# Second attention: the quotient's numerators kept and divided in place in a ring of five units, and its row sums formed one slot group later

## The chip, the cores and the metric

One core of a Trainium2 chip runs the whole program in one launch. The metric is device time in microseconds (us) of that core; lower is better. The kernel before took 3159.86 us (median of 3 runs, 3156.14 to 3160.17).

## The reference, cut to what matters

The program is one hybrid layer on x of shape (4, 512, 512): a first attention with a pairwise sparsity mask, a feed-forward block, a second (differential) attention, the feed-forward block again. Only the second attention is touched. It computes, for each batch b and head h of 16:

```python
attn1 = einsum('bthd,bshd->bhts', q1, k1) * scale
attn2 = einsum('bthd,bshd->bhts', q2, k2) * scale
score = softmax(attn1 - lam * attn2, axis=-1)
out = einsum('bhts,bshd->bthd', score, v)
out = (1.0 - LAMBDA_INIT) * out.reshape(B, T, E)
x = x + out @ W_proj
```

## The kernel before, in words

Each of the five engines (TensorE, VectorE, ScalarE, GpSimd, SyncE) gets its own instruction stream from one list of steps, which `order_of_attention_b` (lines 1778 to 1893) writes out; `attention_b` (lines 1896 to 2274) walks the list and every engine's program emits its share of each step. So the position of a step in the list is its position in each engine's queue.

Work is cut into 16 units: 4 batches times 4 groups of 4 heads (`HU` = 4). A unit has 16 score tiles of 128 x 512. For each tile there are two products: one (`max_b`, matmul L2065, then a row maximum on VectorE, L2168) finds the maxima, and one (`exp_b`, matmul L2080, then the exponential on ScalarE, L2236) gives exp(score - max) transposed. The maxima pass of unit n runs one unit ahead of the exponentials. The list is made in slots, 16 to a unit: slot i of block n holds the exponentials' tile (n-1, i-6) (from i = 6; the slots 0 to 5 still belong to unit n-2), the maxima's tile (n, i), at slots 10, 14, 2 and 6 a `weighted_b` step, and at most one half of a side step. In what follows "slot i" is this i, "class" is n mod 4.

The steps around the change:
- `weighted_b` (t = 0 to 3): 8 matmuls of 32 columns each (L2091) accumulate v times exponentials in one PSUM bank. After t = 3 ScalarE copies this bank, the numerators, to SBUF (L2242).
- GpSimd adds the exponentials over the four t into `ex_sum` (L2018); the adds of the next unit with t = 1 wait until the sums' matmuls have read it (`sums_done`).
- `sums_b`: 8 matmuls of 32 columns against ones (L2103) turn `ex_sum` into row sums, spread over the heads' partitions; ScalarE copies them to SBUF (L2246).
- `divide_b`: 8 pieces of 128 x 64, each a reciprocal (L2177) and a product (L2178) on VectorE, into `out_t`; one piece per odd slot, or in every slot where the block's class is 1.
- `project_b`: for t = 0 to 3 a product with `W_proj` (L2114), in two halves, two slots behind the division of its pieces, once per batch; VectorE adds it to x (L2184).
- `product_b` (L2050), `values_b` (L2038), `turn_b` (L2027) make the queries, keys, values and turned inputs of units to come, in two banks (`SIDE`) that all side steps use in turn; ScalarE makes `hi_b` from a product (L2218) and VectorE `lo_b` (L2160), and SyncE sends both (`send_b`, L2261 and L2265). `place_b` at slot 2 turns the maxima on TensorE (L2072), copies them on ScalarE (L2224), which then issues four DMAs (L2229).

Before, the numerators go to `sums_sb[:, 0]`, the sums to `sums_sb[:, 1]`, and the quotients to `out_t[:, c]`, c = 0 to 3. The numerators' copy therefore waits for the previous unit's last division, and a batch's first division for the previous batch's last projection:

```python
act.wait_ge(divided, 2 * NT * n)          # L2241, before the copy L2242
dve.wait_ge(proj_done, NT * b)            # L2176, before the reciprocal L2177
```

The sums step enters the side queue one slot behind the last weighted sums (slot 7, or slot 8 where a half step is open), the unit's first division right behind it:

```python
if step[2] == NT - 1 and step[1] < UNITS - 1:
    held.insert(0, (m + 1, ("sums_b", step[1])))
```

Behind the last unit, the list ends with `early_b` (the first three quarters of the last batch's projection, L2126), the last weighted sums, sums, divisions and `last_b` (L2131, L2190). `early_b` waits for all divisions of unit 14. The second feed-forward block starts when the last x is added.

Of the kernel before, what the change touches and what calls it, by code (L numbers as in the profile page):

```python
# [7 lines left out]
ACT = mybir.ActivationFunctionType  # L8
# [7 lines left out]
P = 128  # L16
B, S, D = 4, 512, 512
NT = S // P
ND = D // P
# [3 lines left out]
HB, HDB = 16, 16  # L23
# [1749 lines left out]
UNITS_B = HB // HU  # L1773
UNITS = B * UNITS_B
# [3 lines left out]
def order_of_attention_b():  # L1778
    order, side, light, divisions, due, half_done, held = [], [], [], [], [], [], []

    def norms(b):
        return [("norm_b", b, t) for t in range(NT)]

    def turned_steps(b):
        return [("turn_b", b, f) for f in range(ND)] + [("values_b", b, t) for t in range(NT)]

    def divide(n, piece, m):

        order.append(("divide_b", n, piece))
        if n % UNITS_B == UNITS_B - 1 and piece % 2:  # L1790
            held.append((m + 2, ("project_b", n // UNITS_B, piece // 2)))

    def advance():
        if half_done:
            step = half_done.pop()
            order.append((*step, 1))
            if step[0] == "project_b":
                light.append(("stats_b", step[1], step[2]))
            return
        step = side.pop(0)  # L1800
        if step[0] in ("values_b", "product_b", "project_b"):
            order.append((*step, 0))
            half_done.append(step)
            return
        order.append(step)
        if step[0] == "sums_b":
            n, = step[1:]
            divisions.extend((n, piece) for piece in range(2 * NT))
            if n == UNITS - 1:
                divisions.clear()  # L1810
                last = iter([("divide_b", n, piece) for piece in range(2 * NT)])
                order.extend([("early_b", 2), next(last), next(last), next(last), next(last)])
                for t in range(NT):
                    order.append(("last_b", t))
                    order.extend([("early_b", 3)] if t == 0 else [("stats_b", B - 1, t - 1)])
                    order.extend(step for step in (next(last, None), next(last, None)) if step)
                order.append(("stats_b", B - 1, NT - 1))

    def query_key_steps(n):
        return [("product_b", n, 0), ("product_b", n, 1), ("send_b", n)]  # L1820

    order += norms(0)
    side, due = turned_steps(0)[:ND], turned_steps(0)[ND:]
    while side:
        advance()
    side += query_key_steps(0)
    advance()
    order.append(("query_scale",))
    side += query_key_steps(1)
    while side or half_done:  # L1830
        advance()
    side, due = due[:NT // 2], due[NT // 2:]
    while side or half_done:
        advance()
    order.append(("load_projection",))
    order += norms(1)
    rows, own, sums = iter(()), iter(()), iter(())
    query_key = []
    for m in range(TILES * (UNITS + 1) + LAG + HU + 4):
        n, i = m // TILES, m % TILES  # L1840
        if i == 0 and n < UNITS:
            rows = iter([("max_b", n, j) for j in range(TILES)])
            if n % UNITS_B == 0 and n // UNITS_B + 1 < B:
                due += turned_steps(n // UNITS_B + 1)
            share = 0 if n == 0 else NT // 2 + ND if n == 1 else (ND, 0, NT // 2, NT // 2)[n % UNITS_B]
            if n < 2:
                side, query_key = query_key_steps(2)[:3 * (n == 0)] + side, []
            else:
                query_key = query_key_steps(n + 1) if n + 1 < UNITS else []
            side = query_key[:2] + side + due[:share]  # L1850
            due = due[share:]
        if i == TILES // 2 and n % UNITS_B == UNITS_B - 1 and n // UNITS_B + 2 < B:
            light += norms(n // UNITS_B + 2)
        if i == LAG + 1:
            side[:0] = query_key[2:]
            query_key = []
        if i == LAG and 1 <= n <= UNITS:
            own = iter([("exp_b", n - 1, t, g) for t in range(NT) for g in range(HU)])
        if i == (LAG + HU) % TILES and 1 <= n <= UNITS:
            sums = iter([("weighted_b", n - 1, t) for t in range(NT)])  # L1860
        while held and held[0][0] <= m:
            step = held.pop(0)[1]
            if step[0] == "sums_b":
                side.insert(0, step)
            else:
                side.append(step)
        order += [step for step in (next(own, None),) if step]
        if i == 2 and 1 <= n <= UNITS:
            order.append(("place_b", n - 1))
        order += [step for step in (next(rows, None),) if step]  # L1870
        if (i - LAG - HU) % HU == 0:
            step = next(sums, None)
            if step:
                if step[1:] == (UNITS - 1, NT - 1):
                    order += [("early_b", 0), step, ("early_b", 1)]
                else:
                    order.append(step)
                if step[2] == NT - 1 and step[1] < UNITS - 1:
                    held.insert(0, (m + 1, ("sums_b", step[1])))
                elif step[2] == NT - 1:  # L1880
                    side.insert(0, ("sums_b", step[1]))
        if side or half_done:
            advance()
        if divisions and (i % 2 or n % UNITS_B == 1):
            divide(*divisions.pop(0), m)
        if light and (i % 2 == 0 or i < NT):
            order.append(light.pop(0))
    while side or light or half_done:
        if light:
            order.append(light.pop(0))  # L1890
        else:
            advance()
    return order


def attention_b(k):
    nc, d, ps, x = k.nc, k.d, k.ps, k.x
    pe, dve, act, pool, sp, chain = k.pe, k.dve, k.act, k.pool, k.sp, k.dve_chain
    signal = k.flag
    ROWS, N_EX, SCALE = 97, 10, HDB ** -0.5  # L1900
    O1_BANKS, O2_BANKS, SUM_BANK, SIDE = (0, 1, 2), (3, 4), 5, (6, 7)
    LAST_BANKS = O1_BANKS + O2_BANKS[:1]
    order = order_of_attention_b()
# [46 lines left out]
    with ExitStack() as mem:  # L1950
# [10 lines left out]
        v = sb(mem, "vb", [P, 2, NT, D])  # L1961
        ex = sb(mem, "ex_b", [P, N_EX, S])
        ex_sum = sb(mem, "ex_sum", [P, HU, S])
        out_t = sb(mem, "out_t", [P, ND, S])
        sums_sb = sb(mem, "sums_sb", [P, 2, S])
        maxes = sb(mem, "maxes_b", [P, 2, HU, NT])
        max_t = sb(mem, "max_t_b", [HU, 2, S], F32R)
        ones = sb(mem, "ones_b", [P, 32])
# [51 lines left out]
        def tensor(kind, *at):  # L2020
# [85 lines left out]
            elif kind == "project_b":  # L2106
# [4 lines left out]
                    pe.wait_ge(proj_weights, 16)  # L2111
                    side_free(step[:3])
                for c in range(2 * half, 2 * half + 2):
                    s = nc.tensor.matmul(ps[:, bank, :], out_t[:, c, t * P:t * P + P], w_proj[:, c, :], start=c == 0,  # L2114
                                         stop=c == ND - 1)
                if half:
                    s.then_inc(proj_done, 1)
            elif kind == "early_b":
# [4 lines left out]
                if t == NT - 1:  # L2123
                    pe.wait_ge(ex_made, TILES * UNITS)
                for c in range(ND - 1):
                    nc.tensor.matmul(ps[:, LAST_BANKS[t], :], out_t[:, c, t * P:t * P + P], w_proj[:, c, :], start=c == 0,  # L2126
                                     stop=False)
            elif kind == "last_b":
                t, = at
                pe.wait_ge(divided, 2 * NT * (UNITS - 1) + 2 * t + 2)  # L2130
                nc.tensor.matmul(ps[:, LAST_BANKS[t], :], out_t[:, ND - 1, t * P:t * P + P], w_proj[:, ND - 1, :],  # L2131
                                 start=False, stop=True).then_inc(proj_done, 1)

        def vector(kind, *at):
            step = (kind, *at)
# [35 lines left out]
                add_exponentials(dve, nc.vector, ex_added_last, *at, HU // 2, 0)  # L2171
            elif kind == "divide_b":
                n, piece = at
                b, c, part = n // UNITS_B, n % UNITS_B, slice(piece * P // 2, piece * P // 2 + P // 2)
                dve.wait_ge(sums_made, n + 1)
                dve.wait_ge(proj_done, NT * b)  # L2176
                chain(nc.vector.reciprocal(sums_sb[:, 1, part], sums_sb[:, 1, part]))  # L2177
                nc.vector.tensor_tensor(out_t[:, c, part], sums_sb[:, 0, part], sums_sb[:, 1, part],  # L2178
                                        ALU.mult).then_inc(divided, 1)
            elif kind == "project_b" and at[2]:  # L2180
                b, t, half = at
# [15 lines left out]
        def scalar(kind, *at):  # L2197
# [40 lines left out]
            elif kind == "weighted_b" and at[1] == NT - 1:  # L2238
                n, t = at
                act.wait_ge(weighted_done, NT * n + NT)  # L2240
                act.wait_ge(divided, 2 * NT * n)  # L2241
                nc.scalar.activation(sums_sb[:, 0, :], ps[:, SUM_BANK, :], ACT.Copy).then_inc(out_sums, 1)  # L2242
            elif kind == "sums_b":
                n, = at
                act.wait_ge(sums_done, n + 1)
                nc.scalar.activation(sums_sb[:, 1, :], ps[:, side_bank[step], :], ACT.Copy).then_inc(sums_made, 1)  # L2246

        def gpsimd(kind, *at):
            if kind == "exp_b" and (at[0] < UNITS - 1 or at[2] >= HU // 2):
# [88 lines left out]
```

## Time and profile before

| what | value |
|---|---|
| median of the runs | 3159.86 us |
| lowest, highest run | 3156.14, 3160.17 us |
| span of the profiled execution, first to last instruction | 3157.4 us |
| PE, DVE, ACT, POOL busy over the span | 95%, 74%, 56%, 34% |
| mean granted TensorE clock, share of full speed | 0.976 |
| second attention in the span | about 2124 to 2622 us |

The profile gives the span of one execution and no separate total for it; the span is 2.5 us under the median of the runs. PE is the matmul part of TensorE, PEld its weight loads, DVE is VectorE, ACT ScalarE, POOL GpSimd, SP SyncE; a "q" behind an engine means its DMA queue. Busy shares count the modelled time of matmuls, which overlap. "Idle before, releaser" is idle time of that engine directly before an instruction and what ended it.

### The profile page before, as it was taken

How to read it: one execution, taken by the hardware profiler on the slowest of the kernel's cores; microseconds unless marked ns; L12 is line 12 of the kernel's file. 1: busy time of each engine (PE TensorE's matmuls, PEld its weight loads, DVE VectorE, ACT ScalarE, POOL GpSimd, SP SyncE). 2: the span in 40 equal slices, each digit the busy share in tenths (PEclk: the TensorE clock that was granted, in tenths of full speed). 3: DMA queues.
4: the chain of work that ended last, by engine and by line, in shares of the span. 5: the costliest groups of instructions: out<-in, count | busy, mean ns of one | idle time of the engine just before them, and what ended most of it. 6: DMA issues, size and time to landing. Idle time of an engine off the chain costs nothing. (4 is left out here: it accounts for less than half of the span.)

```text
span 3157.4 us, 45069 instructions
## 1 busy us (share of the span) xinstructions
PE 3004.7 (95%) x16681; PEld 1670.8 (53%) x16681; DVE 2335.5 (74%) x4298; ACT 1771.7 (56%) x2897; POOL 1059.2 (34%) x881
## 2 busy tenths in 40 slices
PE   6999999999999899999899989989999987999999
PEld 3334334333433344444478868854444435887787
DVE  6988998999898877777366676655766776667665
ACT  4988888888888546666633333323443443334332
POOL 1000000000000264543155565613545554565653
PEclk9999999999999889999999999999999988999999
DMA  2000000000000000000111111124333311112111
GB/s 75 1 1 11 1 1 11 1 1 11 1 1 1 1 1 2 1 2 1 31 44 54 50 41 57 47 92 109 88 91 77 101 34 53 44 54 74 54 53 44
DMA packets 105759, 112.18 MB, mean 36 GB/s; under 512 B 8963, under 2 KB 74500, under 8 KB 105157
## 3 DMA queue, kind: packets, MB, share of 16 engines
q1 hardware_dynamic: 102918, 108.61, 12.2%
q8 instruction: 134, 2.20, 0.3%
q10 hardware_dynamic: 2624, 0.69, 0.1%
q14 instruction: 83, 0.68, 0.1%
HBM read 84.76 MB, written 20.97 MB: 33 GB/s over the span
## 5 line engine op out<-in xcount | busy, mean ns | idle before, releaser
L730 DVE TENSOR_SCALAR pair_in<-key_words,row_words 128x512 f32<-128x512 f32 x1792 | 726.1, 480 | 44.7 <-PE ps L617 40.7
L815 ACT ACTIVATE pair_mid<-ps,row_bias 128x512 f32<-128x512 f32 x896 | 588.2, 688 | 133.5 <-PE ps L617 116.1
L617 PE MATMUL ps<-pair_in,w_hi 128*64 128x512 f16 x3584 | 584.7, 390 | 8.6 <-DVE pair_in L730 8.3
L1081 DVE TENSOR_REDUCE maxes<-ps 128x2 f32<-128x1024 f32 x256 | 303.2, 1221 | 94.5 <-PE ps L994 93.4
L843 POOL TENSOR_SCALAR_AFFINE_SELECT sim<-sim 128x512 f32<-128x512 f32 x16 | 9.9, 620 | 1051.9 <-ACT sim L832 1051.9
L617 PEld LDWEIGHTS ps<-pair_in,w_hi 128*64 128x64 f16 x3584 | 202.3, 108 | 301.8 <-issue 66.4
L617 PE MATMUL ps<-pair_in,w_lo 128*64 128x512 f16 x1792 | 352.3, 388 | 0.0
L1491 PE MATMUL ps<-ffn_b_hi,ffn_a_hi 128*128 128x512 f32 x904 | 287.6, 400 | 24.8 <-DVE ffn_up L1579 9.9
L1125 ACT ACTIVATE ex<-ps 128x512 f32<-128x512 f32 x448 | 243.2, 595 | 118.2 <-PE ps L1013 117.4
L1491 PE MATMUL ps<-ffn_b_lo,ffn_a_hi 128*128 128x512 f32 x904 | 283.5, 395 | 2.4 <-DVE ffn_b_lo L1561 2.4
L1491 PE MATMUL ps<-ffn_b_hi,ffn_a_lo 128*128 128x512 f32 x904 | 282.8, 394 | 0.7 <-POOL ffn_a_lo L1722 0.7
L1629 DVE TENSOR_TENSOR x<-x,ps 128x512 f32<-128x512 f32 x256 | 175.5, 686 | 138.6 <-PE ps L1508 135.5
L631 PE MATMUL ps<-pair_mid,w_slide 128*32 128x512 f32 x2048 | 246.2, 598 | 0.0
L2236 ACT ACTIVATE ex_b<-ps 128x512 f32<-128x512 f32 x256 | 147.1, 599 | 171.7 <-PE ps L2080 170.5
L2168 DVE TENSOR_REDUCE maxes_b<-ps 128x1 f32<-128x512 f32 x256 | 169.4, 682 | 86.1 <-PE ps L2065 85.6
L1491 PEld LDWEIGHTS ps<-ffn_b_hi,ffn_a_hi 128*128 128x128 f32 x904 | 170.0, 191 | 70.8 <-DVE ffn_up L1579 12.4
L1722 POOL TENSOR_TENSOR ffn_a_lo<-ffn_sums,ffn_a_hi 128x1024 fp32r<-128x1024 f32 x60 | 148.3, 2471 | 171.2 <-ACT ffn_a_hi L1644 171.2
L1689 ACT ACTIVATE ffn_gate<-ffn_gate 128x512 f32<-128x512 f32 x60 | 37.9, 632 | 278.6 <-DVE ffn_gate L1586 278.6
L1491 PEld LDWEIGHTS ps<-ffn_b_lo,ffn_a_hi 128*128 128x128 f32 x904 | 172.1, 191 | 40.8 <-DVE ffn_b_lo L1561 4.2
L1491 PEld LDWEIGHTS ps<-ffn_b_hi,ffn_a_lo 128*128 128x128 f32 x904 | 172.4, 191 | 37.9 <-POOL ffn_a_lo L1722 1.1
L2018 POOL TENSOR_TENSOR ex_sum<-ex_sum,ex_b 128x512 f32<-128x512 f32 x124 | 156.2, 1276 | 85.9 <-ACT ex_b L2236 85.6
L1722 POOL TENSOR_TENSOR ffn_a_lo<-ffn_raw_up,ffn_a_hi 128x512 fp32r<-128x512 f32 (+1 forms) x128 | 136.6, 1089 | 105.9 <-PE ps L1045 67.0
(240 smaller groups left out, 5344.6 us busy)
## 6 DMA issues: line engine op xcount, KB each, us to landing
ffn_raw_up<-in_w_ffn SPq DMA_DIRECT2D x64, 512.0 KB, 4.0
ffn_raw_down<-in_w_ffn SPq DMA_DIRECT2D x64, 256.0 KB, 2.7
q_stack<-halves SPq DMA_DIRECT2D x48, 256.0 KB, 5.1
k_stack<-halves SPq DMA_DIRECT2D x48, 256.0 KB, 5.9
halves<-hi_b SPq DMA_DIRECT2D x16, 512.0 KB, 2.7
halves<-lo_b SPq DMA_DIRECT2D x16, 512.0 KB, 3.6
out<-x SPq DMA_DIRECT2D x4, 1024.0 KB, 4.5
x<-in_x SPq DMA_DIRECT2D x6, 512.0 KB, 6.9
```

The lines of the kernel that those rows point to most:

```text
L617: s = nc.tensor.matmul(ps[F2 * half:F2 * half + F2, bank + which, :], w_part[:, :], words.rearrange("p (s two) -> p s two", two=2)[:, :, o ...
L631: s = nc.tensor.matmul(ps[32 * c:32 * c + 32, 6 + w, :], p.w3_slide[:, 30 - 2 * r:62 - 2 * r], p.pair_mid[:, n % NG, half, :], start=r == ...
L730: s = nc.vector.tensor_scalar(p.pair_in[:, (4 * n + i) % N_PAIR, :], p.key_words[:, b % 2, :], p.row_words[:, b % 2, row:row + 1], None, A ...
L815: nc.scalar.activation(p.pair_mid[:, n % NG, which, :], ps[:, bank + which, :], ACT.Relu, bias=bias).then_inc(p.mid_made, 1)
L1081: nc.vector.tensor_reduce(maxes[:, c % 2, 2 * pair:2 * pair + 2, h], ps[:, 2 * pair:2 * pair + 2, :], AX.X, ALU.max).then_inc(maxes_made, 1)
L1125: nc.scalar.activation(ex[:, i % N_EX, :], ps[:, EXP_BANKS[j], :], ACT.Exp, scale=2.0 ** -0.5).then_inc(ex_made, 1)
L1491: i = nc.tensor.matmul(bank, a_part[:, s % 2, a_at, h, :], b_part[:, place(operand), h, :], start=opens and (which, m, h) == (0, 0, 0), st ...
L1629: nc.vector.tensor_tensor(x[:, n, :], x[:, n, :], ps[:, 6 + t % 2, :], ALU.add).then_inc(x_added, 1)
L1722: nc.gpsimd.tensor_tensor(lo, source, hi.bitcast(F32), ALU.subtract).then_inc(w_lo_made, 1)
L2018: engine.tensor_tensor(ex_sum[:, g, :], first, ex[:, i % N_EX, :], ALU.add).then_inc(done, 1)
L2168: nc.vector.tensor_reduce(maxes[:, n % 2, g, t:t + 1], ps[:, O1_BANKS[i % 3], :], AX.X, ALU.max).then_inc(max_made, 1)
L2236: nc.scalar.activation(ex[:, i % N_EX, :], ps[:, O2_BANKS[i % 2], :], ACT.Exp, scale=SCALE).then_inc(ex_made, 1)
```

## The change

The numerators' copy writes straight into `out_t`, which now has 5 rows of units in a ring; the division works in place there. `sums_sb` keeps the sums alone. The numerators' copy waits no longer for divisions but, from unit 5 on, for the projection that read its place in the ring. The sums' copy now waits for the previous unit's last division, and every division also for its numerators' copy. The `sums_b` step of unit n leaves the side queue and stands directly behind `weighted_b` (n+1, t = 0), at slot 10; the divisions follow from there. For the last unit `sums_b` stays where it was. SBUF in use is the same (4 + 2 rows before, 5 + 1 after).

```diff
@@ order_of_attention_b
         if step[0] == "sums_b":
             n, = step[1:]
-            divisions.extend((n, piece) for piece in range(2 * NT))
             if n == UNITS - 1:
-                divisions.clear()
                 last = iter([("divide_b", n, piece) for piece in range(2 * NT)])
...
         while held and held[0][0] <= m:
-            step = held.pop(0)[1]
-            if step[0] == "sums_b":
-                side.insert(0, step)
-            else:
-                side.append(step)
+            side.append(held.pop(0)[1])
...
-                if step[2] == NT - 1 and step[1] < UNITS - 1:
-                    held.insert(0, (m + 1, ("sums_b", step[1])))
-                elif step[2] == NT - 1:
+                if step[2] == 0 and step[1] > 0:
+                    order.append(("sums_b", step[1] - 1))
+                    divisions.extend((step[1] - 1, piece) for piece in range(2 * NT))
+                if step[1:] == (UNITS - 1, NT - 1):
                     side.insert(0, ("sums_b", step[1]))
@@ attention_b
-    ROWS, N_EX, SCALE = 97, 10, HDB ** -0.5
+    ROWS, N_EX, N_OUT, SCALE = 97, 10, UNITS_B + 1, HDB ** -0.5
...
-        out_t = sb(mem, "out_t", [P, ND, S])
-        sums_sb = sb(mem, "sums_sb", [P, 2, S])
+        out_t = sb(mem, "out_t", [P, N_OUT, S])
+        sums_sb = sb(mem, "sums_sb", [P, S])
...
-                b, c, part = n // UNITS_B, n % UNITS_B, slice(piece * P // 2, piece * P // 2 + P // 2)
+                part, out = slice(piece * P // 2, piece * P // 2 + P // 2), out_t[:, n % N_OUT, :]
+                dve.wait_ge(out_sums, n + 1)
                 dve.wait_ge(sums_made, n + 1)
-                dve.wait_ge(proj_done, NT * b)
-                chain(nc.vector.reciprocal(sums_sb[:, 1, part], sums_sb[:, 1, part]))
-                nc.vector.tensor_tensor(out_t[:, c, part], sums_sb[:, 0, part], sums_sb[:, 1, part],
+                chain(nc.vector.reciprocal(sums_sb[:, part], sums_sb[:, part]))
+                nc.vector.tensor_tensor(out[:, part], out[:, part], sums_sb[:, part],
                                         ALU.mult).then_inc(divided, 1)
...
                 act.wait_ge(weighted_done, NT * n + NT)
-                act.wait_ge(divided, 2 * NT * n)
-                nc.scalar.activation(sums_sb[:, 0, :], ps[:, SUM_BANK, :], ACT.Copy).then_inc(out_sums, 1)
+                if n >= N_OUT:
+                    act.wait_ge(proj_done, NT * ((n - N_OUT) // UNITS_B + 1))
+                nc.scalar.activation(out_t[:, n % N_OUT, :], ps[:, SUM_BANK, :], ACT.Copy).then_inc(out_sums, 1)
             elif kind == "sums_b":
                 n, = at
                 act.wait_ge(sums_done, n + 1)
-                nc.scalar.activation(sums_sb[:, 1, :], ps[:, side_bank[step], :], ACT.Copy).then_inc(sums_made, 1)
+                act.wait_ge(divided, 2 * NT * n)
+                nc.scalar.activation(sums_sb[:, :], ps[:, side_bank[step], :], ACT.Copy).then_inc(sums_made, 1)
```

The projections (`project_b`, `early_b`, `last_b`) read `out_t` at the unit's number modulo 5 in place of c.

## Rows read from the trace of the kernel before

**Rows 1.** The page's head and first part: span, busy time by engine.

```profile
span 3157.4 us, 45069 instructions
...
PE 3004.7 (95%) x16681; PEld 1670.8 (53%) x16681; DVE 2335.5 (74%) x4298; ACT 1771.7 (56%) x2897; POOL 1059.2 (34%) x881
```

**Rows 2.** Busy time by stretch; columns: stretch, length, PE, PEld, DVE, ACT, POOL, clock, DMA, GB/s.

```profile
2124.00:2622.00 498.00, 465.57 (x1732) 203.22 (x1730) 340.70 (x599) 199.50 (x361) 234.31 (x186) 0.96 0.32 83
```

**Rows 3.** Waits in the second attention: who waited for whom, total us, times, longest.

```profile
ACT sums_sb L2242 <- DVE out_t L2178: 25.8, 7, 4.3
...
PE ps L2080 <- ACT ex_b L2236: 10.7, 16, 2.1
DVE sums_sb L2177 <- PE ps L2114: 10.1, 2, 5.1
...
PE ps L2065 <- DVE maxes_b L2168: 6.7, 11, 1.3
```

**Rows 4.** Timeline at the numerators' copies; columns: start, us, engine, line, [idle before].

```profile
2212.51 0.60 ACT L2242 ACTIVATE sums_sb<-ps 128x512 f32<-128x512 f32 x1 [4.28 <-DVE out_t L2178]
...
2237.57 1.07 PE L2103 MATMUL ps<-ex_sum,ones_b 128*32 128x512 f32 x8
...
2239.54 0.60 ACT L2242 ACTIVATE sums_sb<-ps 128x512 f32<-128x512 f32 x1 [3.30 <-DVE out_t L2178]
...
2241.17 0.50 PE L2080 MATMUL ps<-q_stack,k_stack 97*128 97x512 f32 x1 [1.86 <-ACT ex_b L2236]
```

**Rows 5.** Timeline of PE: other idle stretches of over 0.8 us, by what ended them.

```profile
2312.44 0.50 PE L2065 MATMUL ps<-k_stack,q_stack 96*128 96x512 f32 x1 [0.86 <-DVE maxes_b L2168]
...
2365.81 0.51 PE L2080 MATMUL ps<-q_stack,k_stack 97*128 97x512 f32 x1 [1.86 <-ACT ex_b L2236]
...
2486.63 0.50 PE L2080 MATMUL ps<-q_stack,k_stack 97*128 97x512 f32 x1 [2.11 <-ACT ex_b L2236]
...
2564.97 0.64 PE L2103 MATMUL ps<-ex_sum,ones_b 128*32 128x512 f32 x4 [0.86 <-POOL ex_sum L2018]
...
2584.81 0.64 PE L2103 MATMUL ps<-ex_sum,ones_b 128*32 128x512 f32 x4 [1.14 <-POOL ex_sum L2018]
```

**Rows 6.** Busy time by stretch, as rows 2: behind or around three of these idles.

```profile
2243.00:2246.00 3.00, 3.00 (x12) 1.04 (x12) 0.93 (x3) 0.65 (x3) 1.27 (x1) 0.54 1.06 207
...
2364.00:2368.00 4.00, 2.19 (x16) 1.25 (x16) 2.07 (x6) 3.81 (x8) 0.00 (x0) 1.00 0.88 197
...
2487.00:2490.00 3.00, 2.76 (x12) 0.50 (x10) 1.98 (x4) 1.65 (x4) 0.94 (x1) 0.68 1.07 197
```

**Rows 7.** Timeline: one slot without and one with weighted sums, both with side work.

```profile
2274.35 0.80 PE L2080 MATMUL ps<-q_stack,k_stack 97*128 97x512 f32 x1
...
2276.55 0.80 PE L2080 MATMUL ps<-q_stack,k_stack 97*128 97x512 f32 x1
...
2279.93 0.80 PE L2080 MATMUL ps<-q_stack,k_stack 97*128 97x512 f32 x1
```

**Rows 8.** Timeline: from the sums of unit 3 to the first projection.

```profile
2265.75 0.60 ACT L2246 ACTIVATE sums_sb<-ps 128x512 f32<-128x512 f32 x1 [0.78 <-PE ps L2103]
...
2268.28 0.22 DVE L2178 TENSOR_TENSOR out_t<-sums_sb 128x64 f32<-128x64 f32 x1
...
2268.56 1.98 PE L2114 MATMUL ps<-wb_proj,out_t 128*128 128x512 f32 x4
...
2273.95 1.13 DVE L2178 TENSOR_TENSOR out_t<-sums_sb 128x64 f32<-128x64 f32 x1
```

**Rows 9.** Timeline: slot 2 of block 6, maxima placed between two products.

```profile
2287.83 0.75 DVE L2160 SCALAR_TENSOR_TENSOR lo_b<-ps,q_scale,hi_b 128x512 fp32r<-128x512 f32 x1 [1.68 <-ACT hi_b L2218]
...
2288.78 2.43 ACTq L2229 DMA_DIRECT2D q_stack<-max_t_b  x4
...
2288.91 1.98 PE L2050 MATMUL ps<-zb_t,wb_qk 128*128 128x512 f32 x4
```

**Rows 10.** Timeline: PE reaches the end of the last unit.

```profile
2601.66 2.84 PE L2126 MATMUL ps<-wb_proj,out_t 128*128 128x512 f32 x6
```

More of the change, by code:

```diff
@@ L2113, in tensor @@
                 for c in range(2 * half, 2 * half + 2):
-                    s = nc.tensor.matmul(ps[:, bank, :], out_t[:, c, t * P:t * P + P], w_proj[:, c, :], start=c == 0,
-                                         stop=c == ND - 1)
+                    s = nc.tensor.matmul(ps[:, bank, :], out_t[:, (UNITS_B * b + c) % N_OUT, t * P:t * P + P],
+                                         w_proj[:, c, :], start=c == 0, stop=c == ND - 1)
                 if half:
@@ L2125, in tensor @@
                 for c in range(ND - 1):
-                    nc.tensor.matmul(ps[:, LAST_BANKS[t], :], out_t[:, c, t * P:t * P + P], w_proj[:, c, :], start=c == 0,
-                                     stop=False)
+                    nc.tensor.matmul(ps[:, LAST_BANKS[t], :], out_t[:, (UNITS - UNITS_B + c) % N_OUT, t * P:t * P + P],
+                                     w_proj[:, c, :], start=c == 0, stop=False)
             elif kind == "last_b":
@@ L2130, in tensor @@
                 pe.wait_ge(divided, 2 * NT * (UNITS - 1) + 2 * t + 2)
-                nc.tensor.matmul(ps[:, LAST_BANKS[t], :], out_t[:, ND - 1, t * P:t * P + P], w_proj[:, ND - 1, :],
-                                 start=False, stop=True).then_inc(proj_done, 1)
+                nc.tensor.matmul(ps[:, LAST_BANKS[t], :], out_t[:, (UNITS - 1) % N_OUT, t * P:t * P + P],
+                                 w_proj[:, ND - 1, :], start=False, stop=True).then_inc(proj_done, 1)
         def vector(kind, *at):
```

## The prediction

> **What bounds the kernel now.** First the page's head: the span, and which engine is busy [rows 1]. TensorE is busy for 95% of 3157.4 us, so only what lengthens or shortens its stream counts. Then the table by stretch, cut to the second attention [rows 2]: 465.6 of 498 us of TensorE, 340.7 of VectorE, 199.5 of ScalarE. Even here TensorE is the limit, and 498 - 465.6 = 32 us is all its idle time. The change touches no other stage, and the feed-forward block starts when the last x is added, so a microsecond won or lost here is one of the total.
>
> Then the waits [rows 3]. ScalarE waits 25.8 us in 7 pieces for the last division before it may copy the numerators: the largest wait that the change aims at. It is not a gain of 25.8 us. TensorE has its own price of it: it idled 10.7 us in 16 pieces for exponentials. The timeline shows how [rows 4]. At 2212.51, after a wait of 4.28 us, no idle stands on TensorE: it had value products to do. At 2239.54 the same wait of 3.30 us stops it for 1.86 us, since there was no side work but the sums. The same comes back at 2365.81 (1.86) and 2486.63 (2.11) [rows 5]. So of seven waits three reach TensorE, with 5.83 us. The second wait is that of VectorE for the last projection of the batch before, 10.1 us in 2 pieces; behind it the maxima come late, and TensorE idles 0.86 us at 2312.44, the first of four rows alike (two each in blocks 6 and 10, 0.86 to 0.91 us), some 3.5 us out of the 6.7 us of maxima waits [rows 3, 5]. The third is the sums' own wait for GpSimd's adds, 2.0 us in 2 pieces (0.86 and 1.14) [rows 5].
>
> **The change, part by part.**
>
> *Numerators' copy without the wait for divisions.* It takes away 5.83 us of idle at most. ScalarE must still make its 0.60 us copy there, and in slots without side work TensorE runs at ScalarE's pace of one 0.6 us exponential a slot; the sums, which filled part of this time with 1 us of matmuls [rows 4], are no longer there. I take 1.5 us for each of the three, 4.5 us; bounds 3.0 (half) and 5.8. The other four waits give nothing: with side work TensorE is late itself.
>
> *Clock.* Behind two of the three stops the granted clock falls to its lower level (1.2 in place of 2.4 GHz) for part of the next 3 us: means 0.54 and 0.68 [rows 6]. At full speed these stretches hold 3.0 x 0.46 and 3.0 x 0.32 us more, 2.3 us together. Without the stop before them I take 2.0 us; bounds 0 and 3.1, as the fall behind 2487 goes on past its row.
>
> *Divisions without the wait for the projection.* The ring takes away the 10.1 us of VectorE, and with it TensorE's 3.5 us; I take 3.5, bounds 1.7 and 3.5.
>
> *Sums three slots later.* GpSimd's last add of a unit is then several slots old, so both waits for it go: 2.0 us, bounds 1.0 and 2.0. The new cost is on GpSimd: its adds with t = 1 of the next unit start only when the sums are through, some 2 us later than their exponentials. Twelve adds of 1.26 us (234.3 us for 186 [rows 2]) are 15.1 us in a unit of at least 20 us (the last ones, 2565 to 2585 in [rows 5]), and the places they free are wanted six slots later. Cost 0, hidden by GpSimd's 34% load [rows 1]; without that cover the next sums would wait 1:1.
>
> *Two groups of narrow matmuls back to back.* A slot with weighted sums starts its successor 3.38 us later (2276.55 to 2279.93), one without after 2.20 (2274.35 to 2276.55) [rows 7]: a group costs 1.18 us, while its matmuls fill 1.07 [rows 4] and are started over about 1.0. Merged, a second group should cost about 1.0: 0.2 us each for 14 units, 2.8 us; bounds 0 and 4.6 (0.33 each, its entry without side work). The Trainium skill, TensorEngine Tiling (Array Packing), section Key Properties, says that changing the tiling mode drains TensorE, while changing the tile does not; by it each merged pair saves a whole change of mode, and the sum would stand at the upper bound. No row here has two such groups in a row.
>
> *Projection (new wait 1).* For n = 3, 7, 11 the first two divisions follow the sums at once, and the projection stands two slots behind its division, as before. Before, TensorE had after the sums three pairs of score products and the weighted sums, and it arrived at 2268.56, just as the second quotient (2268.28 + 0.22) was ready, 2.75 us after the sums' copy had started (2265.75) [rows 8]. Now the weighted sums stand ahead of the sums, so TensorE arrives 1.0 us earlier and waits; and GpSimd starts its held-back adds at the same moment, under which a product of 128 x 64 takes 1.13 us in place of 0.22 [rows 8]. Cost 1.2 us for each of 3; bounds 0 and 2.4 (both products delayed), so 3.6 us, 0 to 7.2.
>
> *Side steps shift by one slot (new wait 2).* With divisions from slot 10, projection 0 starts at slot 13 and the second half of projection 1 takes slot 0 of the next block (6, 10, 14). So the query product takes slots 1 and 2 and not 0 and 1, and `place_b`, fixed at slot 2, stands before its second half. On ScalarE the maxima's copy and four DMA issues of 2.43 us (2288.78) then stand before the `hi_b` copy, where they stood behind it [rows 9]. The key product shares its bank with the query product and waits for `lo_b`: the issues end at 2291.2, a copy of this size takes 0.60 [rows 4], `lo_b` 0.75 [rows 9], so with the hand-overs between engines `lo_b` ends near 2292.8 and the matmul could start at 2293.1. TensorE arrives one half product and two score products behind 2288.91, 2.2 us by the plain slot [rows 7], at 2291.1. Cost 2.0 us for each of 3, 6.0 us; bounds 0 and 6.6. Before, no idle stood here (2288.91). SyncE's sends move to slot 7 or 8, one or two earlier: no cost.
>
> *Sums' copy waits for divisions; divisions for numerators.* The last division stands at slot 9 or before, the copy needs matmuls that end about 3 us into slot 10: cost 0, with a VectorE lag under 2 us as cover. If VectorE is later than that, ScalarE's exponentials queue behind the copy. The numerators' copy is four slots old when wanted: 0. Copy and product in place have the shapes of before: 0.
>
> *The tail.* Unit 14's divisions end two slots later, at the slot before `early_b` (0), which stands at 2601.66 [rows 10] and waits for them; VectorE also adds for unit 15 there. The idle of 1.14 us before it is counted above. I take 0; bounds 1.5 us of gain (no wait for GpSimd, denser matmuls and a better clock) and 2 us of loss.
>
> **Sum.** Gains 4.5 + 2.0 + 3.5 + 2.0 + 2.8 = 14.8 us; losses 3.6 + 6.0 = 9.6 us; net 5.2 us faster. The profiled span of 3157.4 would be 3152.2; against the median of the runs, 2.5 us above the span, 3154.7.
>
> **Rivals.** *A, new waits are covered.* If `lo_b` and the first quotients come in time (VectorE is idle for a third of the stage [rows 2]), the gains stand alone: 3159.9 - 14.8 = 3145 us, with half of a wait left 3149. For it: before, both places are met to within 0.1 us. Against it: ScalarE is blocked by its own DMA issues, and that doesn't hinge on load. Chance 0.15.
>
> *B, the wait moves.* ScalarE's wait is not removed but moved to the sums' copy, and where no side work stands TensorE runs at ScalarE's pace anyway; the gains of the first two parts go, and the rest cancels against the new waits: 8.3 against 9.6 us, 3159.9 +- 2. For it: four of seven waits cost nothing even now. Against: the last division, which released the copy at 2239.54 [rows 4], falls in slot 9, and the new wait stands some 3 us into slot 10. Chance 0.20.
>
> *C, slower.* One mechanism: TensorE's new stops at the projection and the key product, in blocks 5, 6, 9, 10, 13 and 14, let the granted clock fall, as stops of 1.9 and 2.1 us did in two of three cases [rows 5, 6]. A fall costs about 1.5 us (3 us at half rate). Six of them are 9 us: 3154.7 + 9 = 3163.7. It decides from the point where more than three or four of the six stops fall so. Against: these blocks are full of side work, and at 2365.81 the clock stayed up [rows 6]. The Trainium skill, TensorE: Matmul & The Clock Gate, section Part 1, has the clock set by how busy the engine recently was; the rows agree that the falls stand behind stops. Chance 0.15.
>
> **Numbers.** The forecast case (net gain between 2 and 9 us) has 0.50. A measurement of this kernel tells about 0.2% from no change, 6.3 us, so the case lies on both sides of that line: 0.28 faster, 0.22 same. Faster: 0.28 + 0.15 (A) = 0.43. Same: 0.22 + 0.20 (B) + 0.03 of C = 0.45. Slower: 0.12. The range of 3146 to 3163 us takes in the forecast case, most of A and B and half of C.
>
> **What would show it.** Right: no wait of L2242 for L2178 and none of L2177 for L2114; no idle over 1 us at slot 9 of blocks 4, 8 and 12; no wait of L2103 for GpSimd except in the last unit; clock at full level behind these places; the two narrow groups together at about 2.0 us. New: TensorE idle of 1 to 2.4 us before the first L2114 of batches 0 to 2, and about 2 us before the key product L2050 of blocks 6, 10 and 14. Wrong: a wait of L2246 for L2178 of several us (B), or the second attention as long as before with the clock's mean under 0.95 (C), or neither new wait there (A).

## The result and the profile after

The changed kernel took 3170.99 us (median of 5 runs, 3166.78 to 3172.22) against 3159.86 before; the ratio is 1.0034, 95% interval 1.0022 to 1.0047. It is slower by 0.34%, where 5 us less were forecast, and outside the range.

The page's head and first part, as [rows 1]:

```profile
span 3169.4 us, 45086 instructions
...
PE 2999.3 (95%) x16681; PEld 1673.1 (53%) x16681; DVE 2339.6 (74%) x4298; ACT 1773.6 (56%) x2897; POOL 1061.1 (33%) x881
```

No engine has more to do; the 12 us are waiting time and time at the lower clock. The table by stretch over the same window as [rows 2] (stretch, length, PE, PEld, DVE, ACT, POOL, clock, DMA, GB/s):

```profile
2124.00:2622.00 498.00, 453.42 (x1703) 203.61 (x1701) 334.65 (x574) 198.46 (x358) 234.38 (x186) 0.96 0.32 82
```

TensorE works 12.2 us less in these 498 us than before: the stage now ends later (its last projection starts at 2633.38 and not at 2619.50), so less of it lies in the window. The waits of the stage (who, for whom, total us, times, longest), as [rows 3]. L2075 is the exponentials' matmul (L2080 before), L2060 the maxima's (L2065), L2109 the projection (L2114), L2121 `early_b` (L2126), L2098 the sums (L2103), L2013 GpSimd's adds (L2018), L2173 the division's product (L2178):

```profile
POOL ex_sum L2013 <- PE ps L2098: 102.4, 14, 10.5
...
ACT ex_b L2231 <- POOL ex_sum L2013: 14.5, 12, 2.6
...
PE ps L2060 <- DMA k_stack<-halves: 10.3, 4, 4.3
...
PE ps L2075 <- ACT ex_b L2231: 8.6, 17, 2.2
...
PE ps L2109 <- DVE out_t L2173: 6.4, 3, 2.1
...
PE ps L2045 <- DVE lo_b L2155: 5.8, 5, 1.4
PE ps L2060 <- DVE maxes_b L2163: 5.5, 8, 1.3
...
PE ps L2121 <- DVE out_t L2173: 5.2, 1, 5.2
```

The waits that the change was to remove are gone: no numerators' copy waits for a division, no reciprocal for a projection, and no sums for GpSimd. In their place stand three that were not there or small: the operands' DMA 10.3 us (1.5 before), the first projections 6.4 (0 before), the end 5.2 (0 before). The timeline of PE shows where (start, us, engine, line, [idle before]):

```profile
2248.18 0.53 PE L2060 MATMUL ps<-k_stack,q_stack 96*128 96x512 f32 x1 [2.69 <-DMA k_stack<-halves]
...
2272.46 2.93 PE L2109 MATMUL ps<-wb_proj,out_t 128*128 128x512 f32 x3 [2.14 <-DVE out_t L2173]
2291.54 1.98 PE L2045 MATMUL ps<-zb_t,wb_qk 128*128 128x512 f32 x4 [1.19 <-DVE lo_b L2155]
...
2377.28 0.80 PE L2060 MATMUL ps<-k_stack,q_stack 96*128 96x512 f32 x1 [4.32 <-DMA k_stack<-halves]
...
2572.23 0.50 PE L2075 MATMUL ps<-q_stack,k_stack 97*128 97x512 f32 x1 [1.54 <-ACT ex_b L2231]
...
2613.98 2.08 PE L2121 MATMUL ps<-wb_proj,out_t 128*128 128x512 f32 x2 [5.19 <-DVE out_t L2173]
```

The projection's stop comes back at 2401.97 and 2525.24 (2.13 each), the key product's at 2421.25 and 2544.24 (1.39, 1.19), the DMA's at 2502.67 (2.40). And behind some of the stops the clock falls, in the table by stretch of the 3 or 4 us that follow each:

```profile
2248.00:2251.00 3.00, 2.82 (x4) 1.28 (x5) 2.15 (x5) 0.00 (x0) 1.97 (x2) 0.59 0.00 0
...
2273.00:2276.00 3.00, 3.00 (x5) 1.07 (x4) 1.98 (x6) 0.00 (x0) 0.55 (x1) 0.53 0.40 74
...
2377.00:2381.00 4.00, 3.72 (x6) 1.85 (x6) 1.38 (x3) 0.00 (x0) 0.41 (x1) 0.50 0.00 0
...
2402.00:2406.00 4.00, 4.00 (x6) 1.61 (x6) 2.48 (x6) 0.03 (x1) 1.05 (x1) 0.57 0.91 176
...
2526.00:2530.00 4.00, 4.00 (x14) 1.36 (x12) 2.45 (x6) 0.60 (x1) 0.54 (x2) 0.70 0.22 40
```

Not behind all of them: after the DMA's stop of 2.40 us and after the key product's stops it stays up.

```profile
2502.00:2506.00 4.00, 3.33 (x9) 1.81 (x10) 3.23 (x7) 0.60 (x1) 2.63 (x4) 1.00 0.01 2
```

Where along the stage the time goes shows in SyncE's queue: the first DMA issue that sends a unit's operands, counted from that of unit 0, less the same in the kernel before (worked out from both timelines; the send of unit u stands in block u - 1):

```
unit          6     7     8     9    10    11    12    13    14    15   x complete
after-before +0.1  +2.1  +2.8  +2.8  +6.4  +8.7  +9.3  +9.1  +7.6  +9.6  +14.5 us
```

The steps up for units 7, 11 and 15 hold the projection, its fall and the key product together, since all three stand before that send (for unit 7 at 2272.46, 2291.54 and 2297.11), less the maxima waits that are gone. The step for unit 10 is mostly the DMA's long stop, the last one (4.9) the end. The steps of 0.7 and 0.6 for units 8 and 12 aren't traced to a stop. The one step down (14) is the old stop of 2.11 us at 2486.63 [rows 5] with its clock fall, less a new DMA stop. Ahead of unit 6 nothing was won, although the stop of 1.86 us at 2241.17 [rows 4] is gone: 2.69 us for the DMA took its place. The long stop of 4.32 us is not all the change's: in e4, which has the same steps up to there, it is 1.94 us. Counted from unit 0, as in this table, the stage is 14.5 us longer; against the start of the program its last projection is 13.9 us later, and the two spans differ by 12.0, so some 2 us of these two profiles come back outside the stage.

### The profile page after: what moved, and what is told of

Read it like the earlier page. It is cut to its first block and busy times, and to the rows that moved or that the text cites. A ratio compares the mean times of both kernels' runs of the same rounds, so it can differ in the third digit from the quotient of the medians.

```text
span 3169.4 us, 45086 instructions
## 1 busy us (share of the span) xinstructions
PE 2999.3 (95%) x16681; PEld 1673.1 (53%) x16681; DVE 2339.6 (74%) x4298; ACT 1773.6 (56%) x2897; POOL 1061.1 (33%) x881
## 3 DMA queue, kind: packets, MB, share of 16 engines
q1 hardware_dynamic: 102918, 108.61, 12.2%
## 5 line engine op out<-in xcount | busy, mean ns | idle before, releaser
L2013 POOL TENSOR_TENSOR ex_sum<-ex_sum,ex_b 128x512 f32<-128x512 f32 x124 | 156.8, 1282 | 102.5 <-ACT ex_b L2231 102.5
```

What stands on the lines that cost most here:

```text
L2013: engine.tensor_tensor(ex_sum[:, g, :], first, ex[:, i % N_EX, :], ALU.add).then_inc(done, 1)
```

## The experiments

Each was timed beside the kernel before on the same chip; ratios are to it, with 95% intervals. They fall into three sessions on three chips (e1 to e4, e5 to e8, e9 to e12), in which the kernel before had medians of 3161.2, 3159.8 and 3161.0 us. So kernels of different sessions, and the changed kernel with all of them, are better compared by their ratios than by their medians. The theory after the result: the ring and its waits are sound, and the loss comes from the new order of steps, which sets TensorE still in three kinds of places. The rival: the ring, or the in-place division, costs something itself.

**e1, the ring alone.** The changed `attention_b` with `order_of_attention_b` of before.

> The changed buffers and waits with the order of steps of the kernel before: numerators copied into the ring and divided in place, sums formed at slot 7 or 8. Theory (the loss comes from the order, the ring itself is a gain): no stop of TensorE at the first projections, none at unit 14's divisions, the two waits of ScalarE and VectorE gone; 3154 to 3159 us, where the stacks' DMA takes back part of it in the blocks of class 0. Rival (the ring itself costs, by its in-place product or by the sums' copy waiting for divisions): 3163 us or more.

3157.9 us, ratio 0.9992 (0.9983 to 1.0001). So on balance the ring doesn't cost; what it gains can't be told from nothing. But two kinds of stops are there that the expectation had ruled out, the projections' and the end's; they are smaller than in the changed kernel, and the kernel before has neither:

```profile
2268.94 1.55 PE L2114 MATMUL ps<-wb_proj,out_t 128*128 128x512 f32 x3 [1.11 <-DVE out_t L2178]
...
2371.83 0.50 PE L2065 MATMUL ps<-k_stack,q_stack 96*128 96x512 f32 x1 [1.44 <-DMA k_stack<-halves]
...
2600.82 4.28 PE L2126 MATMUL ps<-wb_proj,out_t 128*128 128x512 f32 x6 [3.12 <-DVE out_t L2178]
```

The projection's stop comes from a shift of 0.07 us between two engines. Before, GpSimd's add starts 0.06 us behind VectorE's second product (2268.28 [rows 8]), and the product takes 0.22 us; in e1 the add starts 0.01 us ahead of the product, which takes 1.33 us. It is so in all three batches of both profiles. Before, then e1:

```profile
2268.34 1.29 POOL L2018 TENSOR_TENSOR ex_sum<-ex_b 128x512 f32<-128x512 f32 x1 [3.78 <-ACT ex_b L2236]
...
2267.55 1.26 POOL L2018 TENSOR_TENSOR ex_sum<-ex_b 128x512 f32<-128x512 f32 x1 [3.77 <-ACT ex_b L2236]
2267.56 1.33 DVE L2178 TENSOR_TENSOR out_t<-out_t,sums_sb 128x64 f32<-128x64 f32 x1
```

The end's stop costs little against the kernel before: that one ran this unit at the lower clock and so arrived just in time (2601.66 [rows 10]), e1 ran it at the upper one and waited. The same stretch, before and in e1:

```profile
2587.00:2600.00 13.00, 12.27 (x34) 3.87 (x35) 9.38 (x18) 5.46 (x11) 5.02 (x4) 0.50 0.00 0
...
2587.00:2600.00 13.00, 8.62 (x36) 2.78 (x36) 11.76 (x20) 7.60 (x14) 7.65 (x6) 1.00 0.01 2
```

**e2, projections one slot later.**

```diff
-            held.append((m + 2, ("project_b", n // UNITS_B, piece // 2)))
+            held.append((m + 3, ("project_b", n // UNITS_B, piece // 2)))
```

> The changed kernel with each projection three slots behind its division and not two, which also puts the query product back on slots 0 and 1. Theory: the stops of 2.1 us before the first projection and of 1.2 to 1.4 us before the key product go in blocks 5, 6, 9, 10, 13 and 14, with the clock falls behind them: 9 to 14 us less than the changed kernel, 3157 to 3162 us. Rival (the loss is the tail and the DMA wait): within 3 us of the changed kernel's 3171 us.

3161.3 us, ratio 1.0000 (0.9991 to 1.0009): this one number takes back the whole loss. The stops before the first projections are down to 0.4 us at most, and the clock doesn't fall there. The key product's stops, expected to go too, are 1.11 us in two of the three blocks: TensorE now reaches it sooner. The DMA's stops (2.44, 4.19, 2.39) and the end's (5.19) are as they were, so the 10 us between the changed kernel and this one don't come from them.

**e3, the maxima placed one slot later in blocks 6, 10 and 14.**

```diff
-        if i == 2 and 1 <= n <= UNITS:
+        if i == 2 + (n % UNITS_B == 2 and n > 2) and 1 <= n <= UNITS:
```

> The changed kernel with the maxima placed one slot later in blocks 6, 10 and 14 alone, so that they again stand between the two products, the projection's wait kept. Theory: only the key product's stop of 1.2 to 1.4 us goes, three times: 3 to 5 us less than the changed kernel, 3166 to 3168 us, and 2.1 us before the first projection stay. Rival (it is ScalarE's DMA issues whatever their slot, or the time is lost elsewhere): no difference from the changed kernel.

3169.0 us, ratio 1.0024 (1.0014 to 1.0035), which overlaps the changed kernel's interval. In its trace the three key products wait 0.66 us each, in place of 1.19, 1.39 and 1.19: the stops are halved and not gone as expected, so about half of each is the order of the maxima's copy and DMA issues. That this saves 2 us fits the medians but isn't settled by them.

**e4, unit 14's divisions in every slot.**

```diff
-        if divisions and (i % 2 or n % UNITS_B == 1):
+        if divisions and (i % 2 or n % UNITS_B == 1 or n == UNITS):
```

> The changed kernel with unit 14's divisions in every slot from slot 10 on, so that they end three slots before the end's first projection part and not one. Theory: the stop of 5.2 us in the last unit shrinks to under 2 us: 3 to 5 us less than the changed kernel, 3166 to 3168 us. Rival (VectorE simply has too much to do there, in whatever order): the stop stays above 4 us and the time within 1.5 us of the changed kernel's.

3168.9 us, ratio 1.0026 (1.0015 to 1.0036), which also overlaps the changed kernel's interval, so a gain is not shown. The stop at the end went from 5.19 to 3.42 us, so it neither went under 2 us as the theory had it nor stayed above 4: VectorE has the work of two units to do behind the late sums.

**e5, a third of the operand copies left out.** From unit 3 on, the third pair of the six DMAs per unit is not made; the scores then miss the keys' low parts of their own unit.

```diff
-                    pe.wait_ge(stacked[n % 3], 16 * 6 * (n // 3 + 1))
+                    pe.wait_ge(stacked[n % 3], 16 * 6 + 16 * 4 * (n // 3))
...
-                for r, (q_half, k_half) in enumerate(((0, 0), (1, 0), (0, 1))):
+                for r, (q_half, k_half) in enumerate(((0, 0), (1, 0), (0, 1))[:3 if n < 3 else 2]):
```

> The changed kernel without the third pair of the six DMAs that fill each unit's score operands (from unit 3 on the rows keep what an older unit left, so the scores miss a correction term). Theory (in blocks 4, 8 and 12 TensorE, freed of ScalarE's wait, arrives before these DMAs have landed): the stops of 2.7, 4.3 and 2.4 us at the first maxima product of the next block fall below 1 us, and the time falls by 5 to 8 us from the changed kernel, to 3163 to 3166 us. Rival (the stop has another cause and moves on): no more than 2 us less.

3159.1 us, ratio 0.9999 (0.9989 to 1.0009), a larger gain than the 5 to 8 us expected. No wait for `k_stack` of over 0.7 us is left, the send of unit 6 comes 3.3 us earlier than before the change, and the clock no longer falls at 2249 and 2375, nor behind the third projection's stop. The stops before the projections stay as they were:

```profile
2266.28 2.73 PE L2109 MATMUL ps<-wb_proj,out_t 128*128 128x512 f32 x4 [2.14 <-DVE out_t L2173]
```

So in blocks 4, 8 and 12 the change did win some 3 us each, and TensorE waited them off at the next block's first product, for operands that go out to memory and come back. This kernel also moves a third less; that it is the time of the way and not the load is borne out by e10, which moves all of it.

**e6, e2 with the end mended.** Unit 14's sums back at slot 7, divisions in every slot of that block.

> The kernel of the second run (projections three slots behind) with the sums of unit 14 back at slot 7 of the last block, and divisions in every slot of that block. Theory: on top of that run's gain the stop of 5.2 us at the last unit goes, and GpSimd's adds of the last unit start earlier: 4 to 7 us less than the second run's 3161 us, 3154 to 3157 us. Rival (the end is bound by GpSimd's adds and the clock there): less than 2 us below the second run.

3158.7 us, ratio 0.9995 (0.9986 to 1.0004): 2.6 us under e2 by the medians, 1.6 by the ratios, short of the 4 expected; the intervals overlap, so a gain on e2 is not shown. The stop of 5.2 us is gone; the last unit runs at the lower clock for 13 us on end:

```profile
2584.00:2597.00 13.00, 11.65 (x35) 3.35 (x34) 7.66 (x18) 5.64 (x10) 3.97 (x4) 0.51 0.00 1
```

The kernel before does the same (0.50 from 2587 to 2600). In e2 the clock is low for about as long, 2582 to 2589 and 2599 to 2606, but there the stop fills 4 us of it. Whether this is what holds e6 back, and whether every run of it does so, is not shown.

**e7, e1 with projections one slot later.** The edit of e2 on the kernel of e1.

> The kernel of the first run (ring alone, order of before) with projections three slots behind, which here shifts the query product by one slot in blocks 6, 10 and 14 and so puts the maxima's copy and DMA issues between the two products: the projection's stop of 1.1 us goes, the stop before the key product of 1.2 to 1.4 us comes. Theory: both stops cost about the same, so within 2.5 us of the first run's 3158 us, with the three stops changed places. Rival (the shift is harmless without the moved sums): 3 us or more below the first run.

3156.2 us, ratio 0.9994 (0.9985 to 1.0003). The three stops of 1.11 us at the projections are gone and 1.19, 1.38 and 1.18 us before the key products have come: the shift by one slot makes them without the moved sums too.

**e8, e1 with the divisions of e4.**

> The kernel of the first run (ring alone, order of before) with divisions in every slot of the last block. Theory: its stop of 3.1 us at the last unit goes, 2 to 4 us less than the first run, 3154 to 3156 us, and so faster than the kernel before by 0.1 to 0.2%. Rival (the stop moves to the sums of unit 15 behind GpSimd): within 1 us of the first run.

3155.6 us, ratio 0.9987 (0.9979 to 0.9996): faster than the kernel before. The end's stop went from 3.12 to 1.42 us and not away. A gain on e1 is not shown, as the intervals overlap.

**e9, GpSimd's adds held.** The changed kernel with one wait more, for units 4, 8 and 12:

```diff
             if t == 1:
                 queue.wait_ge(sums_done, n)
+                if n % UNITS_B == 0 and n > 0:
+                    queue.wait_ge(divided, 2 * NT * (n - 1) + 2)
```

> The changed kernel in which GpSimd's first adds of units 4, 8 and 12 also wait for the first two divisions, so that nothing of GpSimd runs beside VectorE's first two products. Theory (a product of two SBUF inputs waits for the end of GpSimd's add): the product of 1.35 us becomes 0.22 and the stop before the first projection falls from 2.1 to about 1.0 us, 2 to 4 us less in all, 3167 to 3169 us. Rival (the stop is set by the order alone): it stays at 2.1 us and the time at 3171 us or above.

The most telling run. In the changed kernel GpSimd's four held-back adds start at once when the sums are through, and VectorE's second product sits under them; the projection waits for it:

```profile
2268.59 4.96 POOL L2013 TENSOR_TENSOR ex_sum<-ex_b 128x512 f32<-128x512 f32 x4 [4.56 <-PE ps L2098]
...
2271.06 1.35 DVE L2173 TENSOR_TENSOR out_t<-out_t,sums_sb 128x64 f32<-128x64 f32 x1
```

In e9 the adds come behind it, and the same product takes 0.22 us:

```profile
2270.14 0.22 DVE L2175 TENSOR_TENSOR out_t<-out_t,sums_sb 128x64 f32<-128x64 f32 x1
...
2270.41 1.98 PE L2111 MATMUL ps<-wb_proj,out_t 128*128 128x512 f32 x4 [1.01 <-DVE out_t L2175]
...
2270.53 2.50 POOL L2015 TENSOR_TENSOR ex_sum<-ex_b 128x512 f32<-128x512 f32 x2 [7.43 <-DVE out_t L2175]
```

The stops are 1.01 us, as the theory had it. The time is not: 3160.4 us, ratio 0.9998 (0.9990 to 1.0007), 10.6 us less than the changed kernel where 2 to 4 were expected. The table by stretch behind those stops says why (the three projections):

```profile
2271.00:2275.00 4.00, 4.00 (x17) 1.55 (x16) 3.88 (x6) 0.60 (x1) 4.00 (x4) 1.00 0.55 109
2395.00:2398.00 3.00, 3.00 (x14) 1.03 (x13) 2.93 (x5) 0.60 (x1) 3.00 (x3) 1.00 1.08 208
2517.00:2521.00 4.00, 4.00 (x17) 1.50 (x16) 2.68 (x6) 0.60 (x1) 4.00 (x4) 1.00 0.55 107
```

Behind the projections the clock never falls, where in the changed kernel it fell three times out of three. From TensorE's arrival at the projection to the key product behind it the changed kernel takes 2.8, 2.8 and 2.7 us more than e9, of which 1.1 is the stop; together 8.3 us. The other 2.3 of the 10.6 us between the two profiles are the DMA's second stop, 4.32 in one and 1.99 us in the other, which the hold doesn't aim at.

**e10 to e12, a shorter way for the operands.** The send is split: q's two halves go when q is made, k's when k is, and only the copies back wait for both.

```diff
+            if kind == "product_b" and at[2]:
+                n, i, half = at
+                sp.wait_ge(lo_made, 2 * n + i + 1)
+                for half, part in enumerate((hi, lo)):
+                    nc.sync.dma_start(halves[n % 2, half, :, i, :], part[:, i, :].bitcast(F32)).then_inc(
+                        halves_sent[n % 2], 16)
...
-                sp.wait_ge(lo_made, 2 * n + 2)
...
-                for half, part in enumerate((hi, lo)):
-                    nc.sync.dma_start(halves[n % 2, half], part[:, :, :].bitcast(F32)).then_inc(halves_sent[n % 2], 16)
...
```

On e8:

> The kernel of the eighth run (ring alone, order of before, divisions in every slot of the last block), with each product's two halves sent when it is made, q before k, and not all four together. Theory (the blocks of class 0 are bound by the chain product, send to memory, six copies back): the stops of 2.0, 1.3 and about 1 us for k_stack go, 2 to 4 us below the eighth run's 3155.6: 3152 to 3154 us, 0.2 to 0.25% below the kernel before. Rival (twice as many transfers cost what the earlier start gives): 3155 us or more.

3150.1 us, ratio 0.9962 (0.9950 to 0.9974), better than expected. Its stops in blocks 4, 8 and 12 for `k_stack` are gone, and from the last issue of `hi_b` to the first copy back it takes 2.74 us where it took 3.95. Its interval lies clear of e8's. With the hold of e9 on top:

> The tenth run's kernel with the ninth run's hold of GpSimd's adds. Theory: the stops of 1.1 us before the first projections go too, 1 to 3 us below the tenth run. Rival (the late adds hold up ScalarE through the ring of exponentials): no gain on the tenth run or a loss.

3146.9 us, ratio 0.9953 (0.9940 to 0.9966). The stops of 1.1 us at the projections are gone: in the old order the hold removes them whole, so there all of it was GpSimd's. But its interval overlaps e10's and the two spans differ by 0.5 us, so the step from e10 is not shown. On e6, the change's own order with its new stops mended:

> The sixth run's kernel (moved sums, later projections, mended end) with the send split as in the tenth run. Theory: its stops of 2.4, 3.7 and 2.4 us for k_stack shrink to under 1 us each and the time falls by 4 to 7 us from 3158.7, to 3152 to 3155 us: then the change's own order, once its three new stops are mended, is as good as that of before. Rival: the gains end in the next wait (ScalarE for GpSimd's held-back adds), less than 3 us below the sixth run.

3150.1 us, ratio 0.9959 (0.9945 to 0.9972): 8.6 us under e6 by the medians, more than the 4 to 7 expected. Yet stops of 0.78, 2.15 and 1.04 us for `k_stack` remain, twice as long as expected at worst. The moved sums are as good as the old order then, and no better.

## Why the prediction was wrong

The bound was read rightly (the loss is idle or slow-clocked TensorE in the second attention), and so were the waits that go. Two steps failed most: the projection's stop was put at 1.2 us without the clock fall behind it, where stop and fall together cost 3.8 us each time by e9, and the gain at the numerators' copy was booked without asking when the operands of the next block land. The sum failed at these steps:

- *Projection, 1.2 us for each of 3.* The stop was foreseen with both its reasons, arrival 1 us early and GpSimd's adds over VectorE's product. Its size was 2.14 us, near the upper bound of 2.4: three times 0.9 short. e9 shows the two parts: 1.0 us is the order, 1.1 GpSimd. That the ring alone brings the second part (e1) was not foreseen.
- *Its clock fall, left out of the sum.* This is rival C, put at 1.5 us a fall. It was counted as a case apart with a chance of 0.15, while the sum's own rows said that stops of 1.9 to 2.1 us bring falls in two of three cases [rows 5, 6]; a stop at the upper bound of that very term had to carry its fall. By e9, stop and fall above a stop of 1.0 us cost 2.7 to 2.8 us in each of 3 places, 8.3 us in all. The key product's stops were not followed by falls, so C was right in mechanism and half right in place. Its own sign, a mean clock under 0.95, didn't come (0.96 over the 498 us, as before).
- *Numerators' copy, 4.5 us, and the clock, 2.0 us.* The stops went, but in blocks 4, 8 and 12 what is late next was not named: the operands' round trip through memory. It was in the trace: at 2373.04 the first maxima product of block 9 already waited 0.15 us for `k_stack`, so there was nothing to be won ahead of it; a wait of 1.5 us in total was passed over. "SyncE's sends move, no cost" had no landing time worked out for the earlier arrival. e5 shows some 3 us a block behind it. With the 1.5 us step down at unit 14 as all that is seen of it, 5 of these 6.5 us were not there.
- *The tail, 0 with 2 us of loss at worst.* The stop was 5.19 us, and the last stretch of the table above is +4.9. The divisions were placed rightly, but VectorE's load was not added up: eight divisions and six adds behind the late sums, with products and adds of VectorE held by GpSimd's. e4 and e6 take it to 3.4 and 0.
- *GpSimd's late adds, 0.* They hold ScalarE for 14.5 us in 12 pieces (0.4 before), and TensorE behind it 1.54 us at 2572.23 and 2.17 at 2591.27. The cover that the prediction named is missing in the last two blocks, where GpSimd adds without a gap from 2563.85 to 2576.22 and from 2580.49 to 2592.86. But e8, whose sums are not late, has both of these stops as well (1.56 and 2.17 us), so that the late adds cause them is not shown.
- *Key product, 2.0 us each.* The mechanism held (e3 takes half of each stop away, e7 makes them in the old order); the size was 1.19, 1.39 and 1.19 us. In block 6 the matmul starts 1.62 us behind the end of the DMA issues where 1.9 were taken, and TensorE arrives 0.4 us behind that end where 0.1 us before it was taken.
- *Two narrow groups back to back, 0.2 us each.* Right, if a little low. In the changed kernel the pair starts its successor 1.86 us after its own start:

```profile
2306.56 1.06 PE L2086 MATMUL ps<-ex_b,vb 128*32 128x512 f32 x8
...
2307.45 1.04 PE L2098 MATMUL ps<-ex_sum,ones_b 128*32 128x512 f32 x8
...
2308.42 0.30 PEld L2109 LDWEIGHTS ps<-wb_proj,out_t 128*128 128x128 f32 x2 [0.84 <-issue]
```

  The second group adds 0.89 to 0.97 us where a lone one cost 1.18 [rows 7]. By the rule of the Trainium skill (TensorEngine Tiling (Array Packing), section Key Properties) a drain is saved at each pair; what is saved is 0.2 to 0.3 us, so the upper bound of 0.33 is about what it is worth.
- *Waits for the projection, 3.5 us, and for GpSimd, 2.0 us.* Both went from the trace; what that gave in time no run shows by itself.

Rival B's sign, a wait of the sums' copy for divisions, is there once (1.9 us) and harmless. Rival A fell.

What stays open: how much of the 2 us of e3 is real, why e6 gave so little of its stop back, and why the clock fell behind some stops of the same length and not behind others.

## What to carry to other kernels

Where the busiest engine is never far ahead of the others, moving one step by three slots moves every step that hangs on it; write out the new list around each one and price every meeting of two engines anew, with what a third engine does to the slower of them at that moment. A stop of a busy TensorE that nears 2 us must be priced with the clock fall that mostly stands behind it, about as much again; halving such a stop gains more than the half. And before a stop is booked as a gain, look up when the next thing it waits for lands: here a round trip through memory, and shortening it was worth 5.5 us between the medians of e8 and e10 and 7.9 by their ratios, where the ring in the order of before, which removes ScalarE's 25.8 and VectorE's 10.1 us of waits [rows 3], gave nothing clear of noise (e1).

## What the runs showed of the hardware

- In a dense stream a stop of TensorE of 1.0 to 1.1 us left the granted clock at its upper level in every projection of e1, e8, e9 and e10; one of 2.12 to 2.14 us put it at the lower for most of the next 3 us in all three places of the changed kernel, e3 and e4, and in two of three of e5. Over the fourteen profiles, from 2235 to 2551, a fall stands at 1 of 61 stops of 1.0 to 1.5 us and at 23 of 30 stops of 1.9 to 2.8 us (not at 2.40 us in the changed kernel, nor at 2.15 in e12). So the length of a stop makes a fall likely but doesn't decide it.
- VectorE's product of 128 x 64 with two SBUF inputs takes 0.22 us alone and up to 1.36 us when GpSimd adds 128 x 512 at the time; it then ends 0.08 us behind an add. In the changed kernel 67 of the 85 products that start while an add runs take over 0.6 us; the other 18, up to 0.26 us, all start in an add's last 0.2 us. Which of the two starts first decides it: 0.05 us ahead of the add a product takes 0.22 us (before), 0.02 us behind its start 1.33 (e1).
- The send of a unit's operands to memory took 4.0 to 4.5 us in most units of the kernels up to e9 (issue of `hi_b` to the first copy back), 9.0 to 9.3 and 7.1 to 7.5 in units 1 and 2, and 5.2 to 6.5 in a few others, in block 8 of some runs and not of others; between the changed kernel and e4, which don't differ there, that moved a stop from 4.3 to 1.9 us (6.29 and 3.96 us for the send).
